# Router end: the one-hots' product with the tile's constant on GpSimd instead of ScalarE

## What is computed

```python
h = rmsnorm(x, norm_w)                       # 2048 tokens, 512 wide
scores = softmax(h @ gate_w.T)               # 32 experts
topk_w, topk_ids = top_k(scores, 4)          # renormalised over the 4
order = argsort(topk_ids.reshape(-1))        # 8192 (token, expert) pairs by expert
buf[sorted_eid, pos] = h[order // 4]         # rows past the capacity are dropped
out = silu(buf @ w13_gate) * (buf @ w13_up) @ w2     # per expert
routed[token] += out * weight
x = x + routed + shared_expert(h)
```

## Time and profile before

| what | value |
|---|---|
| median of 3 runs | 1132.25 us (1130.59 to 1133.34) |
| the profiled execution | 1129.42 us |
| its span, first to last instruction | 1127.3 us |
| mean granted clock of TensorE | 0.964 of full |
| busy: TensorE, VectorE, ScalarE, GpSimd | 1051.1, 842.9, 485.0, 441.2 us |

### The profile page before, as it was taken

The page is one execution under the profiler, slowest core; times in us unless marked ns, Lnnn a source line. Parts: engine busy times, 40 slices in busy tenths (PEclk is TensorE's granted clock), DMA queues, the critical chain, the costliest instruction groups (busy, mean ns, idle before and its releaser), DMA issues. The chain is left out here.

```text
span 1127.3 us, 21676 instructions
## 1 busy us (share of the span) xinstructions
PE 1051.1 (93%) x6039; PEld 807.7 (72%) x6040; DVE 842.9 (75%) x1588; ACT 485.0 (43%) x1021; POOL 441.2 (39%) x355
## 2 busy tenths in 40 slices
PE   7999789999996989999899988999999999999997
PEld 6999756544443568988787765788887887878873
DVE  5659557969997648787897995868688687766656
ACT  3343335345563368878422163333333333333320
POOL 0000013125541202766861002566666655656620
PEclk9999999999998869999898998999999999999999
DMA  7434450433333677573165314889899899888759
GB/s 282 163 118 177 171 161 1 86 67 70 57 65 87 217 270 243 192 258 123 52 244 185 66 57 159 228 205 265 193 259 261 201 267 256 210 197 189 145 117 373
DMA packets 148381, 195.49 MB, mean 173 GB/s; under 512 B 63177, under 2 KB 80969, under 8 KB 148336
## 3 DMA queue, kind: packets, MB, share of 16 engines
q1 hardware_dynamic: 130704, 156.61, 43.6%
q0 software_dynamic: 17632, 38.32, 17.1%
HBM read 136.57 MB, written 50.34 MB: 166 GB/s over the span
## 5 line engine op out<-in xcount | busy, mean ns | idle before, releaser
L2529 POOL DMA_INDIRECT y_d<-tail,x_ox x78 | 141.2, 1810 | 123.4 <-ACT tail L2773 93.5
L1802 POOL DMA_INDIRECT e_rows<-r_d,x_ix x80 | 102.4, 1280 | 107.4 <-issue 97.6
L2605 PE MATMUL x_h<-x_w_hi,x_t_hi 128*128 x320 | 125.7, 393 | 0.0
L2606 PE MATMUL x_h<-x_w_lo,x_t_hi 128*128 x320 | 125.4, 392 | 0.0
L2607 PE MATMUL x_h<-x_w_hi,x_t_lo 128*128 x320 | 125.1, 391 | 0.0
L1786 DVE TENSOR_TENSOR x_w_lo<-w,x_w_hi (+2 forms) x65 | 112.7, 1734 | 9.3 <-ACT x_w_hi L2747 1.7
L2738 ACT ACTIVATE e_rows<-x_h 128x256 f32<-128x256 f32 x80 | 30.7, 383 | 176.6 <-PE x_h L2607 176.6
L226 POOL TENSOR_TENSOR ln_rstd<-ln_ve,powers 128x2 f32<-128x2 f32 (+1 forms) x40 | 35.3, 882 | 165.3 <-DVE ln_ve L220 165.3
L1786 DVE TENSOR_TENSOR x_t_lo<-x_xb,x_t_hi 128x512 fp32r<-128x512 f32 x79 | 54.6, 691 | 41.1 <-ACT x_t_hi L2733 39.8
L1646 DVE SCALAR_TENSOR_TENSOR raw<-h_qk,h_d 128x768 f32<-128x768 f32 x64 | 58.2, 951 | 26.8 <-PE h_qk L1523 12.9
L2624 PE MATMUL x_o<-x_w_hi,x_avt_hi 128*128 x160 | 73.6, 460 | 1.5 <-issue 1.2
(11 more groups left out here) (438 smaller groups left out, 2659.3 us busy)
## 6 DMA issues: line engine op xcount, KB each, us to landing
w<-in_L_ffn_w SPq DMA_DIRECT2D x32, 1024.0 KB, 8.8
w<-in_L_ffn_w SPq DMA_DIRECT2D x32, 512.0 KB, 8.8
h_negm<-negm_d SPq DMA_DIRECT2D x15, 1024.0 KB, 7.7
raw<-in_L_ffn_w SPq DMA_DIRECT2D x3, 2816.0 KB, 15.6
x_res<-in_x SPq DMA_DIRECT2D x8, 512.0 KB, 5.5
ctx_in<-in_ctx SPq DMA_DIRECT2D x8, 512.0 KB, 3.6
kt_d<-ct SPq DMA_DIRECT2D x8, 512.0 KB, 5.5
vc_d<-ctx_in SPq DMA_DIRECT2D x8, 512.0 KB, 2.6
```

Source lines behind the costliest of these rows:

```text
L1802: nc.gpsimd.indirect_dma_start(out=xg[q][s], out_offset=None, in_=r_d, in_offset=bass.IndirectOffsetOnAxis(ap=ix[q][:, s:s + 1], axis=0), ...
L2529: nc.gpsimd.indirect_dma_start(out=y_d[s], out_offset=bass.IndirectOffsetOnAxis(ap=ox[q][:, s:s + 1], axis=0), in_=eo[q][s][:], in_offset= ...
L2605: nc.tensor.matmul(hbank[s], hi[:, k, :], w13p[0][:, at, k, :], start=k == 0, stop=False)
L2606: nc.tensor.matmul(hbank[s], hi[:, k, :], w13p[1][:, at, k, :], start=False, stop=False)
```

## The change

GpSimd makes the product with t - NT, in a loop over the 16 tiles that stands in its queue behind the four memsets and ahead of the first gathers. ScalarE keeps the product with unit, which now raises hot_ready by itself. A new semaphore, tile_ready, tells of GpSimd's half; TensorE waits for it besides hot_ready, and VectorE does so before it reuses a buffer of ohhi. GpSimd waits once for t_done, since ohs lies over memory of the tail, and from the ninth tile on for hot_used.

```diff
+        tile_ready = sem("rt_tile_ready")
@@ block.gpsimd
                 for s in range(2):
                     nc.gpsimd.memset(xg[q][s], 0.0).then_inc(fills, 1)
+            pool.wait_ge(t_done, 1)
+            for t in range(NT):
+                pool.wait_ge(hi_ready, t + 1)
+                if t >= DEEP:
+                    pool.wait_ge(hot_used, t - DEEP + 1)
+                nc.gpsimd.tensor_scalar(ohs[:, t % DEEP, :, 1, :], ohhi[:, t % HI_DEEP], float(t - NT), 1.0,
+                                        ALU.mult, ALU.mult).then_inc(tile_ready, 1)
             pool.wait_ge(fills, 7)
@@ block.scalar, hot(t)
-                nc.scalar.activation(ohs[:, q, :, 0, :], ohhi[:, t % HI_DEEP], ACT.Copy, scale=unit[:, 0:1])
-                nc.scalar.activation(ohs[:, q, :, 1, :], ohhi[:, t % HI_DEEP], ACT.Copy,
-                                     scale=float(t - NT)).then_inc(hot_ready, 1)
+                nc.scalar.activation(ohs[:, q, :, 0, :], ohhi[:, t % HI_DEEP], ACT.Copy, scale=unit[:, 0:1]).then_inc(hot_ready, 1)
@@ block.tensor, hot(lo_t, hi_t)
                     pe.wait_ge(hot_ready, t + 1)
+                    pe.wait_ge(tile_ready, t + 1)
@@ block.vector, hot(t)
                     dve.wait_ge(hot_ready, t - HI_DEEP + 1)
+                    dve.wait_ge(tile_ready, t - HI_DEEP + 1)
```

## The result

| | before | after |
|---|---|---|
| median of 15 runs each | 1130.96 us (1128.87 to 1133.34) | 1135.88 us (1131.37 to 1140.11) |
| ratio, 95% interval | | 1.0040 (1.0027 to 1.0053) |
| profiled execution, span | 1129.42, 1127.3 us | 1133.66, 1131.5 us |

The change costs 4.9 us by the medians, 0.4% (the interval is 3.1 to 6.0 us). The page's busy shares (answering) move as the work did: ScalarE loses 8 us, GpSimd gains 7, and VectorE, on which nothing was added, gains 4.

A forecast was written before the change was run, and what follows sets the result against it. TensorE's wait for tile 15's product (677.83), behind VectorE's one-hots, was taken as the bound. Start 649.97 + 32.0 of GpSimd products + 13.6 of exclusion = 695.6, +17.8 us: 1150.0 us on the median, range 1135 to 1160.

The forecast's parts named there:

- third rival: GpSimd's product takes 0.96 us but is still shut out by VectorE's one-hots: +2.4 to +8.3 us, chance 0.11.
- The price of the product: GpSimd's new product, priced by L311 at 1.92 us, 2.0 us a tile with the gap.
- It is the new pace maker: While the table is built, GpSimd's 16 products by themselves would end at 682.0 against ScalarE's 677.83: +4.1 us.
- The share of 0.70: GpSimd's products lose 0.70 us per us of wide VectorE work beside them: 19.5 us of one-hots cost 13.6 us.
- second rival: GpSimd works on through the short one-hots, so only its own pace is left: +4.1 us, 1136.4, chance 0.17.
- first rival: VectorE is shut out for all of a product, one-hots and products alternate: +23.6 us, 1155.9, chance 0.28.
- ScalarE's half: ScalarE, rid of 16 products, could end at 676.4 instead of 677.83: -1.4 us at most, if GpSimd's half is ready.
- TensorE's clock: Granted clock around the table's end: nothing added; 0.5 us if the 2.68 us behind the table all ran at 0.5.
- One for one to the end: All behind the last tile's product is in order, so a shift of that moment reaches the kernel's end in full.

The follow-up runs named there:

- e4_forms: The kernel before with twelve more GpSimd TENSOR_SCALARs ahead of its memsets, six forms of operations and types, each twice: 1133.3 us, one execution.
- e11_slow: The changed kernel with the product's second operation, a multiplication by 1, replaced by a minimum with 127: ratio 1.0072 against the kernel before.
- e6_last: The kernel before, but GpSimd makes only the last tile's product with the constant, behind VectorE's last one-hot: ratio 1.0005.
- e8_last_silu: e6_last with ScalarE's silu(7) moved from ahead of the last four tiles to behind them: ratio 0.9987 against the kernel before.
- e2_beside: The kernel before with GpSimd also making the product, into a buffer nobody reads, ScalarE still making both: ratio 1.0042.
- e3_twice: The changed kernel with every product of GpSimd made twice, one behind the other: ratio 1.0083 against the kernel before.
- e14_memset: e2_beside with a memset of the idle buffer (128x512, bf16) in place of the product: 1134.4 us, one execution.
- e5_psum_iota: The changed kernel with VectorE's one-hots comparing an f32 copy of the row in PSUM instead of the bf16 one in SBUF: 1141.8 us, one execution.
- e13_half: e2_beside with GpSimd's idle product over 256 elements a partition in place of 512: 1131.8 us, one execution.
- e10_up: The changed kernel with the first four matmuls of up(7) put between the table's last five tiles: ratio 1.0050 against the kernel before.

## Why the prediction was wrong

It named the direction (slower, 0.91) and the engine pair, but 1150.0 is three to four times too far, and the time came out where the prediction had put its third rival, "quick but shut out", +2.4 to +8.3 us, with a chance of 0.11. That was in part luck. The rival's condition, that L311's length comes of its f32 input, is false, and its sum put GpSimd's products and VectorE's one-hots in a row; VectorE's one-hots and 0.42 us a product are what adds up.

**The price of the product** is the step that failed first: "I take 1.92, since operation, count and output type match". The row I took matched in the name of the instruction, but the name leaves out the two arithmetic operations, and e4_forms shows that these set the price: 0.62 us for two multiplications, 1.92 with subtract and min, whatever the input type. The bounds from below (0.52 and 0.96) did hold 0.62 between them; I chose the other end. The Trainium skill's price (GPSIMD Engine Reference, Performance versus the Vector engine: 512 elements in about 0.77 us in the best loop), which I set aside for L311, was much nearer to the measured 0.617.

**"It is the new pace maker"** fell with it: GpSimd waits 1.1 us before most products. VectorE stays the pace maker, slowed.

**The share of 0.70**, drawn from one meeting of L311 with L376 and L382, failed as a form, not only in size. It made the loss grow with the time that both engines run, and put it on GpSimd. In fact the product hardly stretches (617 to 670 ns) and VectorE pays, 0.42 us a product of 512 elements. With both engines' terms right: 12 x 0.42 = 5.0 in place of 13.6, and GpSimd's 0.62 behind the last one-hot, beside ScalarE's 0.72, in place of 32.0 us in a row. It is also the larger error: e11_slow has the product at 1.97 us, the price I had taken, and costs 7.3 us, not 17.8. So of the 12.9 us between 17.8 and 4.9 some 10 are the share's and some 2.4 the price's. The second rival, "short waits are absorbed" (+4.1), describes that kernel better, if 0.2 us a tile too cheap.

**The first rival**, exclusion for the whole instruction, had the mechanism of the quick product: there the held one-hot ends just behind the product, 0.42 us late, as far as the trace can tell as the earlier trace rows showed it for TENSOR_TENSORs. Its +23.6 us failed by the price, and by its putting products and one-hots in a row though a product follows only every second group of four. For the slow product it fails: e11_slow's one-hots run freely in its middle, 0.4 and 0.13 us being held of 1.97. So the Trainium skill's rule (SBUF — State Buffer, SBUF: two separate sides: an exclusive lock for the whole instruction) agrees with the product of 0.617 us and not with the one of 1.97. L382's going on unharmed in the middle of L311 is of a piece with that; why L311 itself lost 2.31 us there, no run tells.

**ScalarE's half**: "-1.4 us, the most this half of the change can give". It gave 1.47: with one product of 0.72 us a tile ScalarE ends 0.75 us behind the last one-hot in place of 2.26. The condition beside it, that it counts only if GpSimd's half is ready, was met (the last product ends at 679.61, ScalarE's at 679.66).

**TensorE's clock**: I added nothing and named 0.5 us as the most. In the profiled pair it cost 0.9. The bound was mis-sized: the same matmuls take 3.62 us at 0.50, so their 2.68 us before were at a mean of about 0.68, not 0.59. But the 0.9 can't be put down to the change. The granted clock fell somewhere near the table's end in ten of the fourteen profiled executions, and where it fell decides: it was low on up(7) in before, after, e6_last, e8_last_silu and e11_slow (2.68 to 3.62 us), on gate(7) in e2_beside, e3_twice and e14_memset (5.00 to 5.57 us in place of 3.62, up(7) then 1.89), on both in e5_psum_iota and e13_half. It stayed full in the three kernels that move up(7)'s matmuls, and in e4_forms, which doesn't. What sets the place stays open.

**One for one to the end**: not contradicted. The medians differ by 4.9 us where the gathers of the profiled pair differ by 4.7, of which up to 0.9 is the clock of that pair. But the part behind the gather varies by over 2 us between executions, so a shift of 4.7 can't be followed through it in one pair; the agreement to 0.2 us is partly luck. Two profiles with the clock full at the table's end, e10_up for the changed kernel and e4_forms for the kernel before, leave the clock out: there the gather is 3.6 us late (38.37 - 34.77), the one-hots' +5.07 less ScalarE's 1.49. The measured interval at the end, 3.1 to 6.0 us, holds both 3.6 and 4.7. The 12 waits and 16 waits cost nothing that shows.

## What to carry to other kernels

Work moved to an idle engine is not free if the two engines share a way to memory: look for instructions of the receiving engine that today run beside the busy one, and see whose spans grow. The cost hides inside the busy engine's instruction lengths and shows as no wait, so compare the lengths of one line, min, median and max, before and after. Before a difference of a microsecond at one place of two profiles is put down to a change, look for an execution without the change that differs by as much. And a row is a price only if the arithmetic operations match too; where they don't, a short run that times the form by itself is worth more than any argument about types.

## What the runs showed of the hardware that I had not expected

- A GpSimd TENSOR_SCALAR of 128x512 takes 0.62 us with two multiplications and 1.92 to 1.97 with a min in it, on bf16 and on f32 alike (e4_forms, e11_slow).
- What it takes from VectorE's wide one-hots: 0.42 us for 512 elements at 0.617 us and 0.21 for 256 elements at 0.407 us, to the product's end both times. Of a product of 1.97 us, 0.35 to 0.43 us at its start and 0.13 at its end, with free work between (e11_slow). A memset of 512 takes 0.12 (e14_memset).
- One-hots of 128 elements come every 0.163 us from SBUF in bf16 and every 0.26 us from PSUM in f32, where they aren't held at all: 32 groups of four, 1.12 to 1.13 us each (e5_psum_iota). An int32 TENSOR_SCALAR reading SBUF is held in the same run, 0.34 us in place of 0.22.
- The same eight matmul records of up(7) take 1.89, 2.68 or 3.62 us as the granted clock is full, mixed or 0.50, and the first two stand in before and in e4_forms, which have the same order of work there.
